# A two-layer graph network on one core: tables joined by pieces in the last stage, edge groups beside all second-layer tiles, 100 groups in the first pass

## Chip, cores and metric

The kernel runs on one core of one Trainium2 chip. The metric is the device time of one execution in microseconds; lower is better. Times below are from the profiled execution unless the three timed runs are named.

## What is computed

6250 nodes with 128 features, 206250 directed edges sorted by destination, each edge with a weight and 128 attributes.

```python
h = relu(layernorm(x))
# first layer: weighted sum over neighbours
deg = segment_sum(w, row); dinv = rsqrt(deg)
x = x + relu(segment_sum((dinv[row]*w*dinv[col])[:, None] * (h @ kernel)[col], row) + bias)
h = relu(layernorm(x))
# second layer: messages in both directions
fwd  = concat([h[src], edge_attr]) @ W_fwd  + b_fwd     # summed at dst
back = concat([h[dst], edge_attr]) @ W_back + b_back    # summed at src
agg = segment_sum(fwd, dst) + segment_sum(back, src);  agg = agg / (cnt + 1e-7)
y = leaky_relu(agg) + h
x = x + gamma * (y - mean(y)) * rsqrt(var(y) + 1e-5) + beta
```

The products with the weights are moved behind the sums, so the second layer needs, per node, the sum of `edge_attr` over its outgoing edges, the sum of `edge_attr` over its incoming edges, and the sums of `h` over its neighbours.

## The kernel before

**Edge groups.** The edges are cut into 202 groups of 1024 (`GE`, 8 steps of 128 edges). For each step VectorE (DVE) makes a 128x128 comparison of keys, TensorE (PE) multiplies it with the attributes, so that edges of the step with one source are summed, ScalarE (ACT) copies the result to SBUF, and GpSimd (POOL) issues one indirect DMA that adds 128 rows to a table in device memory. There are K = 4 tables (`d.tab_gcn`), used in turn, so a scatter waits for the one four before it. A row holds 256 words: 128 for the first layer's message sums, 128 for the attribute sums (`d.table(k)` is the second half).

**Two passes share the groups.** `first_layer` carries the first `G1` = 104 groups, and their scatters write both halves of a row (L879). It works in 26 half tiles of 64 node pairs: beside the 4 groups (`GPI`) of a half tile PE counts neighbours from one-hots (`pairs`, L1065), turns the counts of the half tile before (`turn`, L1043) and multiplies them with `g` (`product`, L1055), and DVE adds (L965). The order is written out: `slot` runs over 32 steps `c`, group work at each, turns at even ones, pairs at odd ones. Half tiles 0, 1 and 2 stand alone, then comes a loop over two at a time, then half tile 25 and a last slot without groups. `keep_sums` on ACT (L1102) may be two groups ahead of the scatters.

**The second pass.** `dense_sums` carries the other `NB` = 98 groups, whose scatters write the attribute half (L1742). It starts with `PG` = 6 groups beside the counting for tile 0 (32 batches of `pairs`) and the cutting of `h` into three bf16 parts (`cut_chunk`, five times, L1772). Then it runs over 25 tiles of 128 node pairs in 13 blocks: three products with the parts for each of 49 node tiles (L1934), the counting for the next tile (L1893), turns by DMA on ACT's queue (L1992), products back (L1956), adds on DVE (L1878), and beside them 4 groups (`GL`) per tile, 32 steps spread over the blocks. This is so for the first `BT` = 23 tiles; tiles 23 and 24 have no groups. `keep_sums` (L1971) fills a ring of four half groups. Each tile's row sums go out by ACT (L2033) and SP (L1707).

**Joining the tables.** When the last group is scattered, SP loads table 0 into `d.src_attr` (L1721 to L1724), and POOL adds tables 1, 2 and 3 to it by three DMAs that accumulate, each waiting for the one before (L1755 to L1760). `dense_sums` ends when they have landed.

**The last stage.** `last_nodes` works on 50 tiles of 128 nodes in five pieces of ten (`PT`). SP loads, per piece, `row_sums`, `h1` and `x1`, 640 KB each (L2192). PE turns a tile of `src_attr` (L2314) and makes five products into one bank (L2326 to L2335). DVE scales it (L2239), bends it (L2247), adds `h1` (L2256), and per piece takes the mean (L2261), variance (L2265), root and scale (L2270, L2271), and finishes (L2275, L2278). ACT squares and norms. POOL adds beta to `x1` (L2218), one instruction per piece. `load_sums` (L2119) belongs to a branch for other inputs that isn't taken.

## Time and profile before

| | us |
|---|---|
| three timed runs: median (lowest to highest) | 4065.53 (4058.59 to 4067.19) |
| profiled execution: its time | 4063.57 |
| profiled execution: its span | 4061.8 |
| first layer's scatters, first to last start | 443.3 to 2098.4 |
| second pass's scatters, first to last start | 2226.8 to 3824.6 |
| first work of the last stage on PE | 3936.4 |

A row of a timeline gives start, length, engine, line, operation, out<-in, count, and in brackets how long the engine had been idle and what released it. SPq and ACTq are DMA issues. `x832` is a count of instructions. POOL is busy in an indirect DMA while it writes its descriptors; the transfer itself lands later.

### The profile page before, as it was taken

What the parts mean: (1) busy time and instruction counts of PE and PEld (TensorE: products, weight loads), DVE (VectorE), ACT (ScalarE), POOL (GpSimd) and SP (SyncE); (2) the same over time, 40 slices, a digit from 0 to 9 for tenths busy, and PEclk for the clock granted to TensorE, in tenths of its full rate; (3) what the DMA queues carried; (4) which work ended last, traced back from release to release, by engine and by line L of the source; (5) the groups of instructions that cost most, each with busy time, mean ns of one, the idle gap of its engine ahead of it and who ended that gap; (6) DMA issues with size and microseconds to landing.
All of it is one profiled execution on the core that took longest, in us unless ns stands there. A gap on an engine that the chain in (4) does not pass through costs nothing. (4 is left out here: it accounts for less than half of the span.)

```text
span 4061.8 us, 95211 instructions
## 1 busy us (share of the span) xinstructions
PE 3260.1 (80%) x28078; PEld 2702.3 (67%) x28078; DVE 2860.3 (70%) x7842; ACT 1576.2 (39%) x4152; POOL 3035.7 (75%) x1814
## 2 busy tenths in 40 slices
PE   3455698888998889889964699888988889899836
PEld 2454587777777777777744577666766667667626
DVE  9899887777777778777846766666666666666515
ACT  1040455555555555555525233233332333333204
POOL 5778688888888888788850788888888888888610
PEclk9787899999999999999986599999999899999968
DMA  9980687877777778778779589888898989888992
GB/s 167 262 286 16 148 144 139 144 136 142 141 137 144 138 140 144 134 138 146 139 125 251 87 141 144 133 134 135 136 139 128 136 137 137 134 134 136 142 160 77
DMA packets 1032612, 582.11 MB, mean 143 GB/s; under 512 B 607653, under 2 KB 944074, under 8 KB 1032084
## 3 DMA queue, kind: packets, MB, share of 16 engines
q0 software_dynamic: 257584, 174.71, 38.0%
q1 hardware_dynamic: 450376, 320.42, 30.3%
q10 hardware_dynamic: 324124, 80.38, 13.1%
q8 instruction: 278, 4.55, 0.5%
q14 instruction: 250, 2.05, 0.2%
HBM read 282.86 MB, written 238.48 MB: 128 GB/s over the span
## 5 line engine op out<-in xcount | busy, mean ns | idle before, releaser
L1742 POOL DMA_INDIRECT gcn_sums<-shared x784 | 1344.8, 1715 | 381.5 <-issue 194.6
L879 POOL DMA_INDIRECT gcn_sums<-fl_sums,fl_to_i x832 | 1360.6, 1635 | 303.2 <-DMA gcn_sums<-fl_sums,fl_to_i 145.3
L1934 PE MATMUL bank<-ds_counts,ds_parts 128*128 128x256 bf16 x3675 | 620.3, 283 | 74.4 <-ACT ds_row_stage L2033 74.4
L1969 ACT CAST ds_counts<-bank 128x392 bf16<-128x392 f32 x800 | 387.6, 487 | 685.0 <-PE bank L1893 667.5
L1107 ACT COPY fl_sums<-bank 128x256 f32<-128x256 f32 x832 | 313.6, 377 | 603.8 <-PE bank L1034 376.9
L1934 PEld LDWEIGHTS bank<-ds_counts,ds_parts 128*128 128x128 bf16 x3675 | 362.4, 101 | 183.3 <-issue 84.8
L1956 PE MATMUL bank<-ds_turned,ds_now 128*128 128x512 bf16 (+1 forms) x1950 | 475.7, 382 | 7.9 <-DMA ds_turned<-ds_counts 7.4
L1913 PE MATMUL bank<-shared 128*128 128x128 f32 x1568 | 373.0, 322 | 25.2 <-DVE shared L1809 25.1
L917 DVE SCALAR_TENSOR_TENSOR fl_same<-fl_key_b,fl_pat,bank 128x128 f32<-128x128 bf16 x832 | 275.1, 343 | 155.1 <-PE bank L1034 138.6
L1033 PE MATMUL bank<-fl_pay,fl_same 128*128 128x128 f32 x1664 | 335.7, 284 | 50.5 <-issue 32.4
L1029 PEld LDWEIGHTS bank<-fl_sum_hot,fl_attrs 128*128 128x128 f32 x1664 | 253.0, 191 | 171.9 <-issue 108.7
L1911 PE MATMUL bank<-shared 128*128 128x64 f32 x1568 | 285.6, 287 | 95.1 <-DVE attr_sums L1796 93.9
L1878 DVE TENSOR_TENSOR src_sums<-src_sums,bank 128x512 f32<-128x512 f32 (+1 forms) x325 | 212.5, 654 | 209.1 <-PE bank L1956 204.6
L1029 PE MATMUL bank<-fl_sum_hot,fl_attrs 128*128 128x128 f32 x1664 | 311.9, 290 | 49.5 <-DVE attr_sums L902 49.4
L1055 PE MATMUL bank<-fl_turned,fl_g_tile 128*128 128x512 f32 (+1 forms) x676 | 336.9, 580 | 8.7 <-DVE gcn_t L965 7.7
L1065 PE MATMUL bank<-fl_hi_w,fl_lo_hot 128*128 128x98 bf16 x4992 | 287.7, 207 | 61.5 <-DVE fl_hi_w L956 59.3
L1034 PE MATMUL bank<-fl_attrs,fl_same 128*128 128x128 f32 x1664 | 326.8, 279 | 0.0
L956 DVE TENSOR_TENSOR fl_hi_w<-fl_hi_hot,fl_twos 128x784 bf16<-128x784 bf16 x624 | 316.6, 562 | 12.6 <-DVE fl_to_i L930 5.3
L1033 PEld LDWEIGHTS bank<-fl_pay,fl_same 128*128 128x128 f32 x1664 | 262.2, 194 | 91.5 <-issue 76.0
L965 DVE TENSOR_TENSOR gcn_t<-gcn_t,bank 128x512 f32<-128x512 f32 (+1 forms) x338 | 220.8, 653 | 132.8 <-PE bank L1055 129.6
L1893 PE MATMUL bank<-ds_hi_hot,ds_lo_hot 128*128 128x98 bf16 x3200 | 289.0, 214 | 30.2 <-issue 14.4
L1065 PEld LDWEIGHTS bank<-fl_hi_w,fl_lo_hot 128*128 128x128 bf16 x4992 | 256.5, 98 | 84.3 <-issue 69.4
(271 smaller groups left out, 6340.2 us busy)
## 6 DMA issues: line engine op xcount, KB each, us to landing
fl_attrs<-in_edge_attr SPq DMA_DIRECT2D x104, 512.0 KB, 4.7
shared<-in_edge_attr SPq DMA_DIRECT2D x194, 256.0 KB
fl_rel_b<-offset_rows SPq DMA_DIRECT2D x104, 256.0 KB
fl_key_b<-key_rows SPq DMA_DIRECT2D x104, 256.0 KB
gcn_sums<-zeros SPq DMA_DIRECT2D x40, 640.0 KB
shared<-key_rows SPq DMA_DIRECT2D x98, 256.0 KB
gcn_sums<-fl_sums,fl_to_i POOLq DMA_INDIRECT x832
near<-src_float SPq DMA_DIRECT2D x1, 12892.0 KB
```

The source lines that it names most:

```text
L879: nc.gpsimd.indirect_dma_start(out=d.tab_gcn[j % K], out_offset=bass.IndirectOffsetOnAxis(ap=to_i[:, (GPI * kk + gi) % 4, j:j + 1], axis=0 ...
L956: last = nc.vector.tensor_tensor(in_twos(hi_w[:, go % 2, m, :, :]), in_twos(hi_hot[:]), per_pair(hh, 2 + m, go, HH), ALU.mult)
L1029: nc.tensor.matmul(win_bank[:, 0:P], attrs[:, h, jj, :], sum_hot[:, jj, :], start=(jj == 0), stop=(jj == J - 1))
L1033: nc.tensor.matmul(sum_bank[j % 2][:, 0:F], same[:, j, :], pay[:, j // U, j % U, :], start=True, stop=True)
L1034: nc.tensor.matmul(sum_bank[j % 2][:, F:2 * F], same[:, j, :], attrs[:, h, j, :], start=True, stop=True).then_inc(summed, 1)
L1055: nc.tensor.matmul(prod_bank[:, 0:n], g_tile[:, old, :], turned[:, (old + b) % 2, 0:n], start=True, stop=True).then_inc(prod_ready, 1)
L1065: last = nc.tensor.matmul(pair_bank[:, c * HH:(c + 1) * HH], lo_hot[:, go % 2, q, :], hi_w[:, go % 2, m, q, :], start=(m == 0), stop=(m == 2))
L1742: nc.gpsimd.indirect_dma_start(out=d.tab_gcn[j % K].rearrange("n (two f) -> (n two) f", two=2), out_offset=bass.IndirectOffsetOnAxis(ap=to ...
L1913: nc.tensor.matmul(sum_bank[half][:, j % U * F:(j % U + 1) * F], same[:, j, :], attrs[:, half, j % U, :], start=True, stop=True).then_inc( ...
L1934: ins = nc.tensor.matmul(row_bank[:, 0:2 * P], parts[:, tile, s, :], counts[:, h, tile, :, :].rearrange("p b q -> p (b q)"), start=(tile = ...
L1956: ins = nc.tensor.matmul(back_bank[v][:, 0:n].rearrange("f (k p) -> f k p", p=P), now[:, h, half, s, :], by_half[:, half, :, :], start=(ha ...
L1969: nc.scalar.copy(to, pair_bank[batch % B][:, 0:PB * HH].rearrange("p (c k) -> p k c", c=PB)).then_inc(pair_copied, 1)
```

## The change

100 groups are in the first pass: half tiles 0, 1, 2 and 25 (`LIGHT`) have three groups, 24 steps, with the same turns, products and pairs spread over them. The second pass has 102 groups: 4 ahead of tile 0, 4 beside each of tiles 0 to 23, 2 beside tile 24. The join leaves `dense_sums`; POOL only waits there for its scatters. In `last_nodes` SP loads all four tables in pieces of 640 KB; DVE adds the first piece's three parts, POOL those of the other four pieces, each add waiting for the one before. `h1` and `x1` become rings of 3 and 4 pieces, so that there is room for six parts. PE waits for the adds at the first turn of each piece.

The groups' numbers:

```diff
-G1 = GPI * 2 * DS
+LIGHT = (0, 1, 2, 2 * DS - 1)
+G1 = GPI * 2 * DS - len(LIGHT)
 NB = NG - G1
 GL = 4
-PG = 6
-BT = (NB - PG) // GL
+PG = 4
+GL_LAST = NB - PG - GL * (SUPER - 1)
```

In `first_layer`:

```diff
+        def groups_in(i, kk):
+
+            if not isinstance(i, int):
+                return GPI
+            k = 2 * i + kk
+            return 0 if k == 2 * DS else GPI - 1 if k in LIGHT else GPI
...
+        def steps(i, kk):
+
+            return J * (groups_in(i, kk) or GPI)
+
+        def turn_at(i, kk, c):
+
+            return [b for b in range(BLOCKS + 1) if b * steps(i, kk) // BATCHES == c]
+
+        def pairs_at(i, kk, c):
+
+            return [n for n in range(BATCHES) if (2 * n + 1) * steps(i, kk) // (2 * BATCHES) == c]
...
-                for c in range(C):
+                for c in range(steps(i, kk)):
```

In `dense_sums`, the loop of every engine, SP and POOL:

```diff
-            with eng.Fori(1, BT // 2) as i:
...
-            pair_of_tiles(BT // 2, 0, True, False)
-            if between:
-                between()
-            pair_of_tiles(BT // 2, 1, False, False)
-            pair_of_tiles(SUPER // 2, 0, False, True)
+            tile(SUPER // 2 - 1, 0, False)
+            tile(SUPER // 2 - 1, 1, False)
+            tile(SUPER // 2, 0, True)
...
-            def load_table():
-                for k in range(K):
-                    sp.wait_ge(added[k], 16 * (J // K) * NB)
-                sp.dma_start(d.src_attr[:], d.table(0)).then_inc(first_in, 16)
...
-            pool.wait_ge(first_in, 16)
-            for k in range(1, K):
-                if k > 1:
-                    pool.wait_ge(merged, 16 * (k - 1))
-                nc.gpsimd.dma_start(d.src_attr[:], d.table(k), accum_op=ALU.add).then_inc(merged, 16)
-            pool.wait_ge(merged, 16 * (K - 1))
+            for gi in range(GL_LAST):
+                scatter_group(SUPER // 2, 0, gi)
+            for k in range(K):
+                pool.wait_ge(added[k], 16 * (J // K) * NB)
```

In `last_nodes`, in the order SP, POOL, DVE, PE:

```diff
+        ADDS = K - 1
+        PB = 2 * ADDS
...
+            def load_tables(r):
+                sp.dma_start(piece(d.src_attr, r), piece(d.table(0), r)).then_inc(acc_in[r], 16)
+                for k in range(1, K):
+                    n = r * ADDS + k - 1
+                    if n >= PB:
+                        before = n - PB + 1
+                        if before <= ADDS:
+                            sp.wait_ge(first_added, before)
+                        else:
+                            sp.wait_ge(later_added, before - ADDS)
+                    sp.dma_start(part[n % PB], piece(d.table(k), r)).then_inc(part_in[n % PB], 16)
...
+                at_least(sp, sum_ready, PT * (r - H1_RING + 1))
+                sp.dma_start(h1[:, r % H1_RING, :, :], piece(nodes(d.h1), r)).then_inc(h1_in[r], 16)
+                at_least(sp, out_ready, r - X1_RING + 1)
+                sp.dma_start(x1[:, r % X1_RING, :, :], piece(nodes(d.x1), r)).then_inc(x1_in[r], 16)
...
+            load_tables(0)
             for m, a in enumerate((d.w_back[F:2 * F, :], d.w_back[0:F, :], d.w_fwd[F:2 * F, :], d.w_fwd[0:F, :])):
                 sp.dma_start(w[:, m, :], a).then_inc(w_in, 16)
             load(0)
...
             for r in range(1, PIECES):
+                load_tables(r)
                 load(r)
...
+            def add_tables(r):
+                pool.wait_ge(acc_in[r], 16)
+                for n in range(r * ADDS, (r + 1) * ADDS):
+                    pool.wait_ge(part_in[n % PB], 16 * (n // PB + 1))
+                    nc.gpsimd.tensor_tensor(piece(d.src_attr, r), piece(d.src_attr, r), part[n % PB], ALU.add).then_inc(later_added, 1)
+                    pool.wait_ge(later_added, n - ADDS + 1)
+
             for r in range(PIECES):
+                if r + 1 < PIECES:
+                    add_tables(r + 1)
+                if r == 0:
+                    pool.wait_ge(bias_in, 32)
...
+            dve.wait_ge(acc_in[0], 16)
+            for n in range(ADDS):
+                dve.wait_ge(part_in[n], 16)
+                nc.vector.tensor_tensor(piece(d.src_attr, 0), piece(d.src_attr, 0), part[n], ALU.add).then_inc(first_added, 1)
+                dve.wait_ge(first_added, n + 1)
             dve.wait_ge(bias_in, 32)
...
+                if t == 0:
+                    pe.wait_ge(first_added, ADDS)
+                elif t % PT == 0:
+                    pe.wait_ge(later_added, ADDS * (t // PT))
```

The helpers `group`, `in_ring` and `loads` number the groups anew and keep the rings in step; every engine's loop uses them.

## Rows read from the trace of the kernel before

**Rows 1.** The page's first part: busy time of each engine over the span.
```profile
PE 3260.1 (80%) x28078; PEld 2702.3 (67%) x28078; DVE 2860.3 (70%) x7842; ACT 1576.2 (39%) x4152; POOL 3035.7 (75%) x1814
```

**Rows 2.** The view of line L879; min/median/max ns, first and last start; who waited.
```profile
L879 POOL DMA_INDIRECT gcn_sums<-fl_sums,fl_to_i x832: 1552/1567/2079, 443.3 to 2098.4; - x167
...
  ACT fl_sums L1107: 217.7, 158
```

**Rows 3.** Busy time by stretch, first layer: PE, PEld, DVE, ACT, POOL; granted clock, DMA.
```profile
1000.00:1300.00 300.00, 270.09 (x2467) 232.40 (x2466) 231.38 (x703) 161.78 (x439) 245.51 (x151) 0.98 0.78 137
```

**Rows 4.** The timeline of DVE where the first layer ends.
```profile
2101.56 0.29 DVE L965 TENSOR_TENSOR gcn_t<-gcn_t,bank 128x128 f32<-128x128 f32 x1 [0.64 <-PE bank L1055]
```

**Rows 5.** The view of line L1742, the second pass's scatters; who waited.
```profile
L1742 POOL DMA_INDIRECT gcn_sums<-shared x784: 1552/1567/2834, 2226.8 to 3824.6; - x196
...
  ACT shared L1981: 177.0, 93
```

**Rows 6.** The timeline of POOL: scatters 32 and 49 of the second pass.
```profile
2303.78 1.57 POOL L1742 DMA_INDIRECT gcn_sums<-shared  x1 [0.30 <-issue]
...
2337.97 1.55 POOL L1742 DMA_INDIRECT gcn_sums<-shared  x1 [0.30 <-issue]
```

**Rows 7.** The timeline of DVE: the fifth group is prepared while the fourth is summed.
```profile
2296.77 0.17 DVE L1813 SCALAR_TENSOR_TENSOR ds_to_f<-ds_later,ds_to_f 128x8 f32<-128x8 f32 x1
```

**Rows 8.** The view of line L1934: PE's products of tile 0 begin at 2312.9.
```profile
L1934 PE MATMUL bank<-ds_counts,ds_parts x3675: 269/273/421, 2312.9 to 3885.2; 128*128 128x256 bf16 x194
```

**Rows 9.** The timeline of ACT: first two half groups beside tile 0 copied out.
```profile
2325.76 0.59 ACT L1981 COPY shared<-bank 128x512 f32<-128x512 f32 x1
...
2333.59 0.59 ACT L1981 COPY shared<-bank 128x512 f32<-128x512 f32 x1
```

**Rows 10.** Busy time by stretch just before tile 0, columns as in group 3.
```profile
2280.00:2300.00 20.00, 11.54 (x63) 10.88 (x64) 14.28 (x39) 3.89 (x8) 16.33 (x9) 0.50 0.43 66
```

**Rows 11.** The timeline of ACT: ends of tiles 22, 23 and 24.
```profile
3797.25 0.37 ACT L2033 COPY ds_row_stage<-bank 128x256 f32<-128x256 f32 x1 [0.86 <-issue]
3840.41 0.37 ACT L2033 COPY ds_row_stage<-bank 128x256 f32<-128x256 f32 x1 [7.55 <-issue]
3885.53 0.37 ACT L2033 COPY ds_row_stage<-bank 128x256 f32<-128x256 f32 x1 [44.74 <-PE bank L1934]
```

**Rows 12.** The timeline of POOL: the last scatter and the last of three joins.
```profile
3824.61 1.57 POOL L1742 DMA_INDIRECT gcn_sums<-shared  x1 [0.30 <-issue]
...
3905.15 4.37 POOL L1759 DMA_DIRECT2D shared<-gcn_sums  x1 [22.55 <-DMA shared<-gcn_sums]
```

**Rows 13.** The timeline of SP and DVE: the last stage's first load and first scaling.
```profile
3936.81 2.18 SPq L2198 DMA_DIRECT2D n_w<-in_L_gnn_W_back  x2
...
3951.91 0.35 DVE L2239 TENSOR_SCALAR shared<-bank,n_per_count 128x128 f32<-128x128 f32 x1 [10.85 <-DMA n_per_feature<-in_L_gnn_beta]
```

**Rows 14.** The timeline of SP and DVE between the layers: same tables loaded in pieces.
```profile
2107.72 0.34 SPq L1417 DMA_DIRECT2D n_w<-in_L_gnn_kernel  x1
...
2118.14 1.49 DVE L1447 TENSOR_TENSOR n_acc<-n_acc,n_part 128x1280 f32<-128x1280 f32 x1 [9.66 <-DMA n_part<-gcn_sums]
...
2124.84 1.49 DVE L1447 TENSOR_TENSOR n_acc<-n_acc,n_part 128x1280 f32<-128x1280 f32 x1 [0.74 <-DMA n_part<-gcn_sums]
```

**Rows 15.** The view of line L2218, POOL's adds in the last stage.
```profile
L2218 POOL TENSOR_TENSOR n_x<-n_x,n_per_feature x5: 2887/2892/3059, 3951.9 to 3977.2; 128x1280 f32<-128x1280 f32 x5
```

**Rows 16.** The timeline of DVE, last stage: during and between POOL's adds.
```profile
3953.34 0.35 DVE L2239 TENSOR_SCALAR shared<-bank,n_per_count 128x128 f32<-128x128 f32 x1 [1.08 <-PE bank L2335]
3953.60 1.33 DVE L2247 SCALAR_TENSOR_TENSOR n_leaky<-shared 128x128 f32<-128x128 f32 x1
...
3962.22 0.27 DVE L2247 SCALAR_TENSOR_TENSOR n_leaky<-shared 128x128 f32<-128x128 f32 x1
...
3964.09 2.99 DVE L2256 SCALAR_TENSOR_TENSOR shared<-n_leaky,n_h 128x128 f32<-128x128 f32 x1
```

**Rows 17.** The view of line L2261, the mean of each piece.
```profile
L2261 DVE TENSOR_SCALAR n_stat<-n_stat x5: 172/173/173, 3968.5 to 4045.6; 128x10 f32<-128x10 f32 x5
```

More of the change, by code:

```diff
@@ L844, in slot @@
                 k = 2 * i + kk
-                for gi in range(0 if last else GPI):
-                    g, h = group(i, kk, gi), gi % 2
+                for gi in range(groups_in(i, kk)):
+                    g, h = group(i, kk, gi), in_ring(i, kk, gi) % 2
                     at_least(sp, to_ready, g - 1)
@@ L870, in slot @@
             def slot(i, kk, last):
-                for gi in range(0 if last else GPI):
-                    g, h = group(i, kk, gi), gi % 2
+                for gi in range(groups_in(i, kk)):
+                    g, h = group(i, kk, gi), in_ring(i, kk, gi) % 2
                     for j in range(J):
@@ L1072, in slot @@
                 first = isinstance(i, int) and i == 0
-                for c in range(C):
+                for c in range(steps(i, kk)):
                     gi, j = divmod(c, J)
@@ L1127, in slot @@
                 first = isinstance(i, int) and i == 0
-                for c in range(C):
+                for c in range(steps(i, kk)):
                     gi, j = divmod(c, J)
@@ L1573, in dense_sums @@
         U = 4
-        STEPS = GL * J
         RING = 4
@@ L1634, in dense_sums, with groups_in, steps_of @@
         wide = lambda b: min(HB, HI - b * HB)
-        def steps_of(b):
-            return range(STEPS * b // BLOCKS, STEPS * (b + 1) // BLOCKS)
+        def groups_in(i, h):
+            return GL_LAST if isinstance(i, int) and 2 * i + h == SUPER - 1 else GL
+        def steps_of(i, h, b):
+            n = J * groups_in(i, h)
+            return range(n * b // BLOCKS, n * (b + 1) // BLOCKS)
         def behind(i, h, gi):
@@ L1859, in _, with add @@
             dve.wait_ge(src_zeroed, CHUNKS)
-            def add(i, h, beside, last):
+            def add(i, h, last):
                 t = 2 * i + h
@@ L1918, in _, with products @@
                     pairs(0, 0, c, first=True)
-            def products(i, h, beside, last):
+            def products(i, h, last):
                 t = 2 * i + h
@@ L1925, in products @@
                     ahead = [] if last else list(range(3 * b, min(3 * b + 3, BATCHES)))
-                    steps = list(steps_of(b)) if beside else []
+                    steps = list(steps_of(i, h, b))
                     for k in range(wide(b)):
@@ L2005, in _, with copies @@
             keep_now(0, 0)
-            def copies(i, h, beside, last):
+            def copies(i, h, last):
                 t = 2 * i + h
@@ L2012, in copies @@
                     ahead = [] if last else list(range(3 * b, min(3 * b + 3, BATCHES)))
-                    steps = list(steps_of(b)) if beside else []
+                    steps = list(steps_of(i, h, b))
                     for n in range(max(len(ahead), len(steps))):
```

156 lines of the change are left out of this document (70 added, 86 removed).

## Prediction, made before the changed kernel ran

> **What bounds the kernel now.** The page's first part [rows 1] comes first: PE 80%, POOL 75%, DVE 70% of one span. Three engines so close say nothing yet, because the stages have different limits. So the views of the two scatter lines come next. In the first layer 832 scatters start from 443.3 to 2098.4 [rows 2]: 1655.1 / 831 = 1.992 us from one to the next, where the instruction alone has a median of 1.57. ACT, which may run two groups ahead, waited 217.7 us for scatters to land. PE is busy 270 of 300 us there [rows 3]: near its limit, but behind POOL. The second pass is alike: 784 scatters from 2226.8 to 3824.6, ACT waiting 177.0 us for them [rows 5]. POOL's queue of scatters sets both passes; a group of eight costs 8 x 1.992 = 15.9 us in the first.
>
> Behind the passes lies a stretch without scatters. The last ends at 3826.2 [rows 12], tile 22 had been finished by PE and ACT at 3797.3, tiles 23 and 24 follow at 3840.4 and 3885.5 [rows 11]. The joins go on: the last starts at 3905.15 [rows 12], and SP issues the last stage's first load at 3936.81 [rows 13]. From scatter to stage: 110.6 us, of which joins alone fill the last 51.
>
> **Part 1, four groups fewer in the first layer.** 4 x 15.9 = 63.7 us less if POOL stays the bound in the light half tiles. What they have besides groups (turns, products, pairs) is packed into 24 steps instead of 32. A half tile lasts 4 x 15.9 = 63.7 us and PE is busy in 0.90 of it, 57.4; the light one has 47.8 us of scatters. Half tile 0 has no turns or products, so PE can build its lead of two groups there, and that covers 1 and 2. After half tile 25 PE has a slot of turns and products without groups; DVE ended it at 2101.85 [rows 4], within 2 us of the last scatter's end at 2099.95, so what PE loses in this half tile shows. I take **-62**. Ends: -64 if PE never shows; if PE's 57.4 us did not shrink at all, each light half tile would save 6.3 and the four -25. ACT's and DVE's orders move with PE's and are bounded by the same two.
>
> **Part 2, the second pass.** Until its 32nd step the start is unchanged. The fourth group's last scatter ends at 2303.78 + 1.57 = 2305.35 [rows 6]. By 2296.8 DVE has prepared the fifth group [rows 7], which is now tile 0's first, so PE can begin tile 0 near 2297 and not at 2312.9 [rows 8]. The first half group of tile 0 was copied out at 2325.76 + 0.59, 13.4 us after tile 0's start, the next 7.8 us later [rows 8, 9]. So the fifth group's scatters begin near 2310.7, after 5.3 us of POOL with nothing; half groups every 7.8 us then feed a POOL that needs 8.1. The clock is granted at 0.50 before tile 0, that is 1.2 GHz, where PE had been busy 11.5 of 20 us [rows 10]; if tile 0's first blocks ran at half the pace, 13 us more would be lost.
>
> From scatter 49 at 2337.97 [rows 6] to 3826.2 are 92 groups: 16.18 us each. Now 98 groups start at 2310.7: 2310.7 + 98 x 16.18 = 3896.3. Tile 24 has two groups; alone it took 45.1 us [rows 11], and PE is 29 us ahead of the scatters at a tile's end (3826.2 - 3797.3), so its last half group is ready about when POOL has reached it. POOL's new wait at the end has nothing queued behind it but the stage's end. After the first layer's last scatter the next stage's first load came 7.8 us later (2107.72 - 2099.95) [rows 2, 14]; so here at 3904.1 instead of 3936.8: **-33**. SP loses one wait and one load. Ends: -38 with no idle POOL, -20 with the 13 us.
>
> **Part 3, the last stage.** Now SP issues four table loads ahead of everything. The same tables' other halves, in pieces of the same size, are joined between the layers: DVE's adds started at 2118.14 and, three later, at 2124.84 [rows 14], 2.23 us per piece. The first scaling on DVE came 15.1 us after the first load, waiting for gamma and beta at the end of the first loads [rows 13]; four pieces ahead make it 15.1 + 8.9 = 24.0. DVE's three adds of 1.49 (the fourth piece plus one add lands near 16) and PE's wait for them hide under that; all 50 tiles stand behind this wait, and they need gamma and beta anyway. So **+9**.
>
> Then POOL has 12 adds more. Its five adds of 2.89 us [rows 15] show what they cost DVE: an operation on two SBUF inputs that takes 0.27 took 1.33 and 2.99 while POOL was adding, ending as POOL did; scaling out of a bank went through in 0.35 beside it [rows 16]. The other three blocked operations lie between these, so 1.06 to 2.72 us lost per add.
>
> The Trainium skill (SBUF — State Buffer, the rules on engine contention) says that DVE with two SBUF inputs and a GpSimd instruction that reads SBUF share a port pair by an exclusive lock, held for the whole instruction of whichever comes first. By that rule every new add could block DVE for all its length, 12 x 2.89 = 34.7 us, an estimate from the rule and the row; this speaks against moving the adds to POOL.
>
> The rows have DVE free part of the time. A piece of the stage is seven loads, 7 x 2.23 = 15.6 us; POOL works 4 x 2.89 = 11.6 of them, from about +28 to +88 after the first load. In each add one tile gets through DVE (one bend, one sum between two adds); in the 4 free us about three: 7 tiles per 15.6 us, and with the five operations per piece besides, near 27 us a piece. Now a piece takes (4045.6 - 3968.5) / 4 = 19.3 [rows 17]. In 60 us: 2.2 pieces instead of 3.1, so 0.9 x 19.3 = **+17**. Ends: 0, if the idle time of DVE in the 19.3 swallowed it all, and 12 x 3.06 = +37. SP's waits for part buffers are for adds a piece earlier, and the h1 and x1 rings wait for pieces three and four earlier; behind them are only loads of pieces that DVE reaches later. Loads at 15.6 a piece stay ahead of DVE.
>
> **Sum.** -62 - 33 + 26 = -69 us on the profiled execution's 4063.6: 3994.6. Its span is 4061.8, 1.8 less; the three runs' median is 4065.5, 1.9 more. Against the median: **3996.5**. Some 8 us (0.2%) is what a measurement of this kernel can tell from no change.
>
> **Rivals.**
> - *Light half tiles give less.* PE, busy in 0.90 of the time [rows 3], becomes their bound. For it: 57.4 of 63.7 us. Against: only a quarter of the groups leaves, and the lead covers three of four. At half the gain, -31: 4027. Chance 0.13.
> - *The lock costs all it can.* +9 + 37 instead of +26: 4016. For it: the 2.99 row; against: the 1.33 row. Chance 0.17. This is the outcome under the skill's rule above.
> - *DVE's idle time swallows the adds.* +9 alone: 3979. For it: POOL finished its adds at 3980 and the stage went on to 4062 at an unchanged 19 us per piece. Chance 0.14.
> - *Slower: the adds stretch.* Place: POOL in the last stage, the last-stage pieces waiting on the adds. POOL's add now has two full pieces as inputs, where one was a broadcast row, and each adds' successor waits for it. Parts 1 and 2 gain 95 and the start costs 9, so it decides at 86 / 12 = 7.2 us per add on the path; at 10 us, +120, the time is 4065.5 - 95 + 9 + 120 = 4100. Against: 2887 to 3059 ns in all five [rows 15]. Chance 0.03.
> - *The groups are moved and nothing else.* A group costs 15.9 in one pass and 16.2 in the other, and if the freed half tiles gave nothing (part 1 at -10) the rest is -33 + 26: 4049. Chance 0.03.
>
> **Numbers.** The forecast has 0.50. Ends: part 1 -64 to -25, part 2 -38 to -20, part 3 +9 to +46; all at once 3972.5 and 4066.5. The range 3972 to 4032 holds the forecast, the lock, the swallowed adds and half-gained half tiles, leaving out the corner where several ends meet. Faster by over 0.2%: 0.93; within: 0.03; slower: 0.04.
>
> **What will show it.** Right: L879's scatters at 1.99 us apart and ending some 62 us earlier; a POOL gap of about 5 us before scatter 33 of the second pass; the last stage's first load about 8 us after the last scatter; first scaling near +24; long L2247 and L2256 operations wherever POOL adds, and early pieces near 27 us apart, late ones near 19. Wrong: gaps on L879 that end with ACT in half tiles 0 to 2 or 25; a longer gap at tile 0; PE waiting for a load or for an add at a piece's first turn; POOL adds longer than 3.1 us.

## The result and the profile after

The changed kernel takes 4034.3 us (median of six runs, 4022.1 to 4044.3), the kernel before 4059.7 in the same runs: ratio 0.9934, 95% interval 0.9917 to 0.9951. It is faster, but by 0.7% and not by the 1.7% forecast; 4034.3 lies just above the range. The profiled execution took 4032.6 us with a span of 4030.6, 31.2 less than before; the forecast for that difference was 69. Times of the experiments below are medians of four executions, with the lowest and the highest, unless one execution is named; one of e13's four took 9519.5 us and is left out of its figures.

The first part of the page has the same three busy engines [rows 1]:

```profile
PE 3246.0 (81%) x27950; PEld 2693.9 (67%) x27950; DVE 2890.0 (72%) x7841; ACT 1576.3 (39%) x4096; POOL 3030.5 (75%) x1823
```

The first layer's scatters are now line L904. Its view in the changed kernel (instruction, then what its idle time ended with, then who waited for it):

```profile
L904 POOL DMA_INDIRECT gcn_sums<-fl_sums,fl_to_i x800: 1552/1553/2077, 445.8 to 2055.2; - x160
...
  issue: 161.4, 473
  ACT fl_sums L1135: 98.2, 130
...
  ACT fl_sums L1135: 50.1, 78
```

Against [rows 2]: ACT's waiting for scatters has fallen from 217.7 to 50.1 us, and POOL sits 98.2 us idle until ACT has copied a sum. The queue of scatters has stopped being the bound; the chain through PE is. The layer's last add, by the timeline of DVE:

```profile
2078.42 0.29 DVE L990 TENSOR_TENSOR gcn_t<-gcn_t,bank 128x128 f32<-128x128 f32 x1 [0.64 <-PE bank L1082]
```

Against 2101.56 [rows 4] that is 23.1 us earlier, where the last scatter came 43.2 earlier: before, DVE's last add stood within 2 us of the last scatter's end, now 22 us behind it. The timeline of POOL, from the first layer's last scatter to the last stage:

```profile
2055.16 1.55 POOL L904 DMA_INDIRECT gcn_sums<-fl_sums,fl_to_i  x1 [0.30 <-issue]
...
2198.80 1.55 POOL L1765 DMA_INDIRECT gcn_sums<-shared  x1 [142.08 <-ACT shared L1999]
...
2282.11 1.55 POOL L1765 DMA_INDIRECT gcn_sums<-shared  x1 [4.23 <-ACT shared L1999]
...
3860.91 1.55 POOL L1765 DMA_INDIRECT gcn_sums<-shared  x1 [0.30 <-issue]
...
3898.59 3.04 POOL L2242 TENSOR_TENSOR shared<-shared,n_part 128x1280 f32<-128x1280 f32 x1 [24.36 <-DMA n_part<-gcn_sums]
...
3913.69 8.94 POOL L2242 TENSOR_TENSOR shared<-shared,n_part 128x1280 f32<-128x1280 f32 x3 [2.91 <-DMA n_part<-gcn_sums]
...
3945.45 11.23 POOL L2242 TENSOR_TENSOR shared<-shared,n_part 128x1280 f32<-128x1280 f32 x3 [4.01 <-DMA n_part<-gcn_sums]
3956.75 5.91 POOL L2251 TENSOR_TENSOR n_x<-n_x,n_per_feature 128x1280 f32<-128x1280 f32 x2
```

So the second pass begins at 2198.8 and not 2226.85: 28.1 us are what is left of part 1 there. Its scatters end at 3862.5; the last stage's first load comes 8.7 us later, by SP's timeline:

```profile
3871.19 0.41 SPq L2200 DMA_DIRECT2D shared<-gcn_sums  x1
```

From the first scatter of the pass to that load are 1672.4 us, where 1710.0 lay before (3936.81 - 2226.85): 37.6 less. From there to the end of the span: 159.4, before 125.0: 34.4 more. Sum: -28.1 - 37.6 + 34.4 = -31.3. The last stage by the timeline of DVE: first scaling (after the wait for gamma and beta), two tiles beside POOL's adds, the mean of each piece (L2294), and a scale (L2304) and a finish (L2311) beside adds:

```profile
3894.03 0.61 DVE L2272 TENSOR_SCALAR shared<-bank,n_per_count 128x128 f32<-128x128 f32 x2 [7.10 <-DMA n_per_feature<-in_L_gnn_beta]
...
3898.78 2.99 DVE L2289 SCALAR_TENSOR_TENSOR shared<-n_leaky,n_h 128x128 f32<-128x128 f32 x1
...
3901.70 0.34 DVE L2272 TENSOR_SCALAR shared<-bank,n_per_count 128x128 f32<-128x128 f32 x1
3901.97 2.76 DVE L2280 SCALAR_TENSOR_TENSOR n_leaky<-shared 128x128 f32<-128x128 f32 x1
...
3916.97 2.72 DVE L2294 TENSOR_SCALAR n_stat<-n_stat 128x10 f32<-128x10 f32 x1
...
3932.92 2.59 DVE L2304 TENSOR_TENSOR n_stat<-n_stat 128x10 f32<-128x10 f32 x1
...
3945.70 2.73 DVE L2294 TENSOR_SCALAR n_stat<-n_stat 128x10 f32<-128x10 f32 x1
...
3949.86 4.08 DVE L2311 TENSOR_TENSOR shared<-shared,n_x 128x1280 f32<-128x1280 f32 x1
...
3977.42 0.17 DVE L2294 TENSOR_SCALAR n_stat<-n_stat 128x10 f32<-128x10 f32 x1
...
3997.20 0.17 DVE L2294 TENSOR_SCALAR n_stat<-n_stat 128x10 f32<-128x10 f32 x1
...
4014.37 0.17 DVE L2294 TENSOR_SCALAR n_stat<-n_stat 128x10 f32<-128x10 f32 x1
```

The first scaling comes 22.8 us after the first load (15.1 before); the pieces then stand 28.7, 31.7, 19.8 and 17.2 us apart, 19.3 on average before [rows 17].

### The profile page after: what moved, and what is told of

Same layout as the page of the kernel before. It is cut to its first block and busy times, and to the rows that moved or that the text cites. A ratio compares the mean times of both kernels' runs of the same rounds, so it can differ in the third digit from the quotient of the medians.

```text
span 4030.6 us, 94845 instructions
## 1 busy us (share of the span) xinstructions
PE 3246.0 (81%) x27950; PEld 2693.9 (67%) x27950; DVE 2890.0 (72%) x7841; ACT 1576.3 (39%) x4096; POOL 3030.5 (75%) x1823
## 5 line engine op out<-in xcount | busy, mean ns | idle before, releaser
L1765 POOL DMA_INDIRECT gcn_sums<-shared x816 | 1392.1, 1706 | 413.7 <-issue 200.0
L904 POOL DMA_INDIRECT gcn_sums<-fl_sums,fl_to_i x800 | 1282.9, 1604 | 335.3 <-issue 161.4
L1135 ACT COPY fl_sums<-bank 128x256 f32<-128x256 f32 x800 | 300.5, 376 | 498.8 <-PE bank L1061 438.9
L1931 PE MATMUL bank<-shared 128*128 128x128 f32 x1632 | 381.3, 317 | 23.0 <-DVE shared L1827 20.9
L942 DVE SCALAR_TENSOR_TENSOR fl_same<-fl_key_b,fl_pat,bank 128x128 f32<-128x128 bf16 x800 | 264.9, 342 | 165.6 <-PE bank L1061 149.5
L1929 PE MATMUL bank<-shared 128*128 128x64 f32 x1632 | 295.2, 285 | 91.1 <-DVE attr_sums L1814 89.9
L1060 PE MATMUL bank<-fl_pay,fl_same 128*128 128x128 f32 x1600 | 322.5, 284 | 38.8 <-issue 38.3
L1061 PE MATMUL bank<-fl_attrs,fl_same 128*128 128x128 f32 x1600 | 315.5, 280 | 0.0
L1929 PEld LDWEIGHTS bank<-shared 128*128 128x128 f32 x1632 | 243.4, 201 | 103.3 <-DVE attr_sums L1814 100.4
L990 DVE TENSOR_TENSOR gcn_t<-gcn_t,bank 128x512 f32<-128x512 f32 (+1 forms) x338 | 220.7, 653 | 126.1 <-PE bank L1082 125.0
L647 PE MATMUL bank<-col_w,row_hot 128*128 128x200 bf16 x1616 | 188.4, 288 | 152.2 <-DVE col_w L560 152.2
```

What stands on the lines that cost most here:

```text
L904: nc.gpsimd.indirect_dma_start(out=d.tab_gcn[j % K], out_offset=bass.IndirectOffsetOnAxis(ap=to_i[:, in_ring(i, kk, gi), j:j + 1], axis=0) ...
L1060: nc.tensor.matmul(sum_bank[j % 2][:, 0:F], same[:, j, :], pay[:, j // U, j % U, :], start=True, stop=True)
L1765: nc.gpsimd.indirect_dma_start(out=d.tab_gcn[j % K].rearrange("n (two f) -> (n two) f", two=2), out_offset=bass.IndirectOffsetOnAxis(ap=to ...
L1929: nc.tensor.matmul(win_bank[:, 0:W], attrs[:, jj // U, jj % U, :], sum_hot[:, jj, :], start=(jj == 0), stop=(jj == J - 1))
L1931: nc.tensor.matmul(sum_bank[half][:, j % U * F:(j % U + 1) * F], same[:, j, :], attrs[:, half, j % U, :], start=True, stop=True).then_inc( ...
```

## The experiments

Half tiles are measured on POOL, from the first scatter of one to the first of the next (us), the last of them to the end of its last scatter. "Even" and "odd" are the means over the full half tiles 6, 8, ... 24 and 5, 7, ... 23; the loop over two half tiles turns ahead of every odd one. "Layer" runs from the first scatter to DVE's last add. Second stop: does PE stand still twice at a turn of the loop (below)?

| kernel (light half tiles) | 0 | 1 | 2 | even | odd | 25 | layer | second stop |
|---|---|---|---|---|---|---|---|---|
| before (none) | 66.8 | 65.4 | 62.6 | 64.2 | 63.3 | 60.3 | 1658.5 | no |
| before, again: r1 | 65.4 | 62.9 | 63.6 | 63.6 | 63.7 | 60.6 | 1653.0 | no |
| changed (0, 1, 2, 25) | 52.4 | 50.8 | 53.2 | 62.4 | 65.7 | 49.8 | 1632.9 | yes |
| e1 (1, 2, 25) | 65.5 | 46.4 | 47.6 | 63.2 | 62.4 | 45.7 | 1601.6 | no |
| e2 (none) | 65.4 | 62.0 | 61.9 | 63.1 | 62.2 | 60.3 | 1633.0 | no |
| e8 (2, 25) | 65.2 | 63.0 | 46.3 | 63.0 | 65.4 | 47.8 | 1654.2 | yes |
| e5, one-hots earlier | 48.8 | 46.9 | 48.6 | 63.2 | 64.7 | 45.9 | 1611.3 | yes |
| e10, 32 transposes | 52.9 | 50.3 | 53.3 | 63.3 | 63.0 | 45.6 | 1606.9 | no |
| e15, 64 transposes | 48.5 | 51.2 | 53.3 | 63.0 | 63.4 | 45.0 | 1602.7 | no |
| e16, 16 transposes | 50.1 | 50.7 | 53.3 | 62.9 | 66.7 | 49.1 | 1646.4 | yes |
| e13, as e5 and e10 together | 50.9 | 46.4 | 47.5 | 62.5 | 63.1 | 45.7 | 1591.1 | no |
| e18, e6 and 72 transposes | 62.8 | 47.0 | 47.1 | 63.3 | 66.8 | 46.5 | 1654.8 | yes |
| e19, 128 transposes | 47.7 | 51.2 | 53.3 | 62.8 | 66.0 | 49.1 | 1635.0 | yes |

**Which half tiles are light (e1, e2, e8).** The theory at that point: without a full half tile 0, PE has no lead over the scatters. The edit, with the counts that hang on it (the 3 in `group`, `in_ring` and `loads` becomes the number of light half tiles ahead of the loop; tiles 23 and 24 of the second pass share what is left):

```diff
-LIGHT = (0, 1, 2, 2 * DS - 1)
+LIGHT = (1, 2, 2 * DS - 1)      # e1; () in e2, (2, 2 * DS - 1) in e8
```

> Half tile 0 of the first layer gets its fourth group back (light half tiles 1, 2 and 25; 101 groups in the first layer, 101 in the second pass, one of them beside the last tile). My theory: in the changed kernel PE and DVE, not the scatters, set the pace of half tile 0 (three groups in 53.1 us there, four in 53.8 us in the kernel before), so the fourth group costs the first layer about 1 us and takes 16 us out of the second pass: about 15 us less than the changed kernel, 4017 against its profiled 4032, with the first layer's last DVE add within 2 us of 2078.7. Rival, the scatters bind it as forecast: the group costs 15.9 us there and saves 16.2 us here: 4032, the first layer ending near 2094.

e1 took 3995.4 us (3991.4 to 3998.7; ratio to before 0.9858, 0.9832 to 0.9884): one group more in the first layer, and the layer is 31 us shorter. Its light half tiles last 46.4, 47.6 and 45.7 us: the 47.8 that the forecast gave for one. So the price of a light half tile was right, as long as a full one stands ahead of it. But the gain (39 us) is more than twice the 15 that my theory expected, so something else went with it.

> Part 1 undone: no light half tiles, 104 groups in the first layer as before; 98 in the second pass, with four ahead, four in each of tiles 0 to 22, two in tile 23 and none in tile 24. My theory: the first layer ends some 23 to 28 us later than in the changed kernel, near 2102 to 2106, as in the kernel before; the second pass's scatters end some 65 - 25 = 40 us earlier, but tiles 23 and 24 then stand alone on PE (45 us each in the trace of before), so the last stage begins within 5 us of where it begins now: 4032 +- 8. Rival, each group was worth 15.9 us in the first layer: it ends near 2078.7 + 62 = 2141 and the whole takes some 35 us longer, 4067.

e2 took 4009.1 us (3991.8 to 4011.6; 0.9892, 0.9866 to 0.9917): 25 us less than the changed kernel with part 1 undone, outside both expectations. So in this kernel the four groups were better left in the first layer. Two steps of mine failed. Tile 24 without groups took PE 32 us and not 45. And the first layer took 1633.0 us with instructions that are the same on every engine as in the kernel before; the repeat, r1, says that the kernel before has 1653 to 1658 in two profiles.

> The kernel before once more, unchanged, for one more profile: the run without light half tiles has the same instructions in its first layer, yet took 1633.0 us from the first scatter to the last DVE add where the profile of before shows 1658.5. If executions differ in the pace of the scatters, this one lies anywhere from 1630 to 1665, its full half tiles near 62.6 to 63.7 us; if something in the changed kernel's placement makes it faster, it is 1655 to 1662 again.

r1: 4059.2 us (one execution), layer 1653.0, within its broad expectation. Executions differ (e2's profiled one was 16 to 20 us faster than its other three), but there is more to it. Between 660 and 2000 us the scatters stand 1.99 us apart in both profiles of the kernel before and 1.96 in e2; in the kernels below with light half tiles it is 1.96 to 1.97 where the loop has one stop at a turn, and 1.98 and 1.99 with four half tiles to a turn (e3, e9). So a full half tile differs by up to 1 us from kernel to kernel without a light half tile in it, the layer by some 20 us. Why the same instructions ran quicker in e2 was not settled.

> Half tiles 2 and 25 alone are light: one group is taken out ahead of the loop (an odd number, as the three of the changed kernel), and half tile 0 is full; 102 groups in the first layer, 100 in the second pass, none of them beside tile 24. Theory, it is the light half tile 0 that costs PE's lead: the full half tiles last 62 to 64 us without alternating, the first layer ends 14 to 16 us after that of the kernel with 1, 2 and 25 light (2043.9), near 2059; the second pass is up to 16 us shorter, less what tile 24 shows alone: 3993 to 4006. Rival, the odd number makes the half tiles alternate: 62 and 67, the first layer ending near 2085, the whole above 4015.

e8 took 4025.8 us (4017.4 to 4029.7; 0.9924, 0.9907 to 0.9940), the rival's outcome. Half tile 0 is full, and yet from half tile 13 on the odd ones last 66 to 69 us. So a lead is built, and then something uses it up. What that is stands in PE's waits between 660 and 2000 us (total, times, longest), here in the changed kernel:

```profile
PE bank L1060 <- issue: 38.3, 10, 5.0
...
PE bank L1092 <- issue: 16.7, 10, 2.6
```

in the kernel before

```profile
PE bank L1033 <- issue: 32.4, 10, 3.6
```

and in e8

```profile
PE bank L1063 <- issue: 43.7, 10, 5.0
...
PE bank L1046 <- issue: 21.9, 10, 3.1
```

Ten turns of the loop, ten stops in which PE waits for nothing that the profile shows. The kernel before has one of 3.2 us at each turn; the changed kernel and e8 have a second one a few us behind it. In PE's timeline of the changed kernel:

```profile
976.40 0.48 PE L1060 MATMUL bank<-fl_pay,fl_same 128*128 128x128 f32 x2 [3.37 <-issue]
976.72 0.39 PE L1061 MATMUL bank<-fl_attrs,fl_same 128*128 128x128 f32 x2
976.94 0.78 PE L1070 MATMUL bank<-ident,fl_mat 128*128 128x128 f32 x4
977.51 0.64 PE L1060 MATMUL bank<-fl_pay,fl_same 128*128 128x128 f32 x2
977.94 0.63 PE L1061 MATMUL bank<-fl_attrs,fl_same 128*128 128x128 f32 x2
978.37 1.91 PE L1043 MATMUL bank<-fl_window,fl_spread_hot 128*128 128x128 f32 x8
980.08 0.62 PE L1092 MATMUL bank<-fl_hi_w,fl_lo_hot 128*128 128x98 bf16 x5
983.29 0.48 PE L1092 MATMUL bank<-fl_hi_w,fl_lo_hot 128*128 128x98 bf16 x7 [2.60 <-issue]
```

2 + 2 + 4 + 2 + 2 + 8 + 5 = 25 matmuls after the turn PE stops again, within a run of twelve that wait for nothing. Two theories: the odd number of groups taken out (three, one) shifts the pairs of groups against the half tiles; or PE's code stands in another place.

**The loop's turns (e3, e10, e11, e14 to e19).**

```diff
-            with eng.Fori(2, DS) as i:
-                slot(i, -1, False)
-                slot(i, 0, False)
+            slot(2, -1, False)
+            slot(2, 0, False)
+            with eng.Fori(0, (DS - 3) // 2) as two:
+                for i in (2 * two + 3, 2 * two + 4):
+                    slot(i, -1, False)
+                    slot(i, 0, False)
```

> The changed kernel with four half tiles to a turn of the first layer's loop, not two, so that the loop turns 5 times and not 11. Theory: with half tile 0 light, PE and DVE have no lead over the scatters, and the 3 to 5 us that PE stands still at each turn of the loop show; six turns fewer take 15 to 30 us off the first layer (DVE's last add near 2050 to 2064, not 2078.7), the whole 4004 to 4019. Rival, the full half tiles alternate between 62 and 67 us because an odd number of groups was taken out ahead of the loop, so that pairs of groups straddle half tiles: the alternation stays, the first layer ends within 5 us of 2078.7.

e3 took 3982.9 us (3976.3 to 3991.3; 0.9820, 0.9797 to 0.9842), the layer 1598.7: more than expected, because the four stops that are left between 660 and 2000 us are single, and the alternation is gone with an odd number still taken out. That speaks against the odd number. The next edit changes nothing but the place of PE's code; its result is not used:

```diff
+            for _ in range(32):     # 64, 16, 128 in e15, e16, e19; 72, 16 in e18, e17
+                nc.tensor.transpose(turn_bank[:, 0:P], d.ident[:], d.ident[:])
             spread(0, 0, 0, 0)
```

> The changed kernel with 32 transposes more on PE ahead of the first layer, whose result is not used, in time in which PE waits. They move the code of PE's loop by as many instructions as one group has: its turn then stands where it stands in the kernel with half tiles 1, 2 and 25 light. Theory, the place of the loop's code decides whether PE stands still once (3.3 us) or twice (4 + 2.5 us) at each turn: full half tiles last 62 to 64 us without alternating, the first layer gets 20 to 30 us shorter (1603 to 1613, not 1632.9), the whole 4003 to 4014. Rival, the odd number of groups taken out makes them alternate, whatever the place: 4030 +- 8 and the alternation as before.

e10 took 4013.8 us (4008.0 to 4020.0; 0.9899, 0.9878 to 0.9921): 20 us less than the changed kernel, for 32 useless transposes. The layer is 26.0 us shorter, the odd half tiles last 63.0. Its waits have one stop per turn (no second row for matmuls that wait for "issue"):

```profile
PE bank L1060 <- issue: 38.9, 10, 4.6
```

> The kernel with half tiles 1, 2 and 25 light and the adds on DVE, with the same 32 transposes ahead of the first layer, which put PE's loop where it stands in the kernel with 2 and 25 light. Theory, place of the code: PE stands still twice at each turn, the lead over the scatters shrinks until the half tiles alternate between 63 and 67 us, the first layer takes 1615 to 1632 us, not 1604.8, the whole 3986 to 4004, not 3976. Rival, odd number of groups: two were taken out, so nothing changes: 3976 +- 5.

e11 took 3977.3 us (3973.5 to 3988.6) beside 3976.4 without the transposes: no change, the rival's outcome. So place alone, as I had counted it (by groups of 32 matmuls), was wrong; four more shifts tell what the place means.

> The kernel with half tiles 2 and 25 light (one group taken out ahead of the loop; PE stood still twice at each turn, 65.2 us in all stops of 1.6 us or more) with the 32 transposes ahead. If the place of PE's loop decides in every kernel that takes an odd number out, as it did in the changed kernel: one stop per turn, some 40 us in all, no alternation, the first layer 1620 to 1632 us, not 1654.2. If the changed kernel was an exception: two stops, 1650 again.

> The changed kernel with 64 transposes ahead, not 32. If what counts is the place of the loop in blocks of 64 PE instructions, this is where the changed kernel stood: two stops a turn, the alternation, the first layer 1625 to 1640 us. If any shift away from the changed kernel's place helps (or the 7 us of PE work ahead does): one stop, 1600 to 1613.

> The changed kernel with 16 transposes ahead. Half way between the two places: if the second stop appears gradually with the place, stops of some 45 us in all and a first layer of 1610 to 1625 us; if it is there or not, either 1600 to 1613 or 1625 to 1640.

> The kernel with half tiles 1, 2 and 25 light and the adds on DVE, with 16 transposes ahead. Where an even number of groups is taken out, a shift by 32 had changed nothing. If no place matters there: one stop per turn of 2.7 to 3.9 us, first layer 1600 to 1610. If it was only that place: a second stop, first layer 1615 to 1630.

One execution each. e14: 3994.2 us, one stop, layer 1619.8. e15: 4016.3, one stop, layer 1602.7. e16: 4056.2, two stops, the second one 11 matmuls behind the turn and not 25, layer 1646.4, 6 us above its range. e17: 3981.4, one stop, layer 1607.2. PE's timeline of e16 behind a turn:

```profile
720.32 0.79 PE L1060 MATMUL bank<-fl_pay,fl_same 128*128 128x128 f32 x2 [4.06 <-issue]
720.90 0.63 PE L1061 MATMUL bank<-fl_attrs,fl_same 128*128 128x128 f32 x2
721.33 1.06 PE L1070 MATMUL bank<-ident,fl_mat 128*128 128x128 f32 x4
722.18 0.63 PE L1060 MATMUL bank<-fl_pay,fl_same 128*128 128x128 f32 x2
722.61 0.42 PE L1061 MATMUL bank<-fl_attrs,fl_same 128*128 128x128 f32 x1
726.97 0.58 PE L1061 MATMUL bank<-fl_attrs,fl_same 128*128 128x128 f32 x1 [3.93 <-issue]
```

That ruled out blocks of 64 PE instructions, and gave a scale: 16 transposes move the second stop 14 matmuls closer to the turn; with 32 and 64 it is gone. In the traces a transpose is two instructions, a weight load and a matmul. In e8 the second stop stands 14 matmuls behind the turn. From this the last two runs were foretold:

> The kernel with half tiles 1, 2 and 25 light and the adds on DVE, with 72 transposes ahead. Theory: PE's code comes in blocks of 256 instructions (a transpose is two, a load of weights and a matmul), and a block that ends within the first 30 matmuls of the loop costs a second stop at each turn. In the changed kernel the second stop lies 25 matmuls behind the turn, with 16 transposes ahead 11, with 2 and 25 light (two groups more) 14: so a group is some 139 instructions, here the end lies 83 matmuls behind the turn, and 72 transposes bring it to about 11 (5 to 17). Two stops per turn, over 55 us in all, half tiles alternating between 63 and 67, the first layer 1615 to 1635 us and a start up to 8 us later. Rival, an even number taken out never shows it: one stop, 1600 to 1610.

> The changed kernel with 128 transposes ahead, that is 256 instructions. Theory: the same place in a block as without them: two stops per turn, the second 25 matmuls behind the turn (21 to 29), the alternation, some 1625 to 1640 us from the first scatter to the end of the first layer, its start up to 20 us later. Rival, any shift of more than 16 removes it: one stop, 1600 to 1613.

In both the second stop came, close to the place foretold; e18's layer did not stay in its range. e18, an even number taken out, PE's timeline behind a turn:

```profile
1112.61 0.79 PE L1063 MATMUL bank<-fl_pay,fl_same 128*128 128x128 f32 x2 [4.64 <-issue]
1113.19 0.63 PE L1064 MATMUL bank<-fl_attrs,fl_same 128*128 128x128 f32 x2
1113.62 1.06 PE L1073 MATMUL bank<-ident,fl_mat 128*128 128x128 f32 x4
1114.47 0.63 PE L1063 MATMUL bank<-fl_pay,fl_same 128*128 128x128 f32 x2
1114.89 0.63 PE L1064 MATMUL bank<-fl_attrs,fl_same 128*128 128x128 f32 x2
1118.55 1.86 PE L1046 MATMUL bank<-fl_window,fl_spread_hot 128*128 128x128 f32 x7 [3.02 <-issue]
```

The second stop stands 12 or 13 matmuls behind the turn (the stretch shows seven of eight matmuls of L1046), 11 foretold; the odd half tiles last 66.8, the layer 1654.8, 50 us more than without the transposes (20 more than I had allowed), the kernel 4026.6. e19, with 256 instructions ahead, is back at the changed kernel's place; its timeline:

```profile
1241.82 0.38 PE L1092 MATMUL bank<-fl_hi_w,fl_lo_hot 128*128 128x98 bf16 x5
1244.97 0.76 PE L1092 MATMUL bank<-fl_hi_w,fl_lo_hot 128*128 128x98 bf16 x7 [2.77 <-issue]
```

again after five of the twelve, 25 matmuls behind the turn; layer 1635.0, kernel 4047.2. So the place of PE's loop counts, with a period of 256 instructions: a shift by 256 brings the second stop back to its matmul, shifts by 64 and 128 (e10, e15) do not. That PE's code comes in pieces of 256, and that each turn costs a second stop where a piece ends shortly behind the start of the loop, is the reading that foretold both runs; no trace shows the pieces themselves. An odd or even number has no part in it, nor has the work of the transposes: e19 has the most of it and gains nothing.

**One step of slack in the light half tiles (e5).** With three groups, DVE's weighing stands one step ahead of the pairs on PE that use it, with four, two. In half tile 0 of the changed kernel (450 to 496 us) PE's waits say:

```profile
PE bank L1092 <- DVE fl_hi_w L981: 8.9, 7, 3.1
```

```diff
-                        if not last and c == full * (go - 1) + full - 2:
+                        if not last and c == full * (go - 1) + full - (2 if full == GPI else 3):
                             one_hots(k, hh, go)
-                        if not last and c == full * (go - 1) + full - 1:
+                        if not last and c == full * (go - 1) + full - (1 if full == GPI else 2):
```

> In the four light half tiles alone DVE builds each set of one-hots one step earlier, so that between the weighing and the pairs on PE that use it lie two steps, as in a full half tile, and not one. Theory, PE and DVE wait for each other in turn in the light half tiles (PE waited 8.9 us for the weighing in half tile 0): each light half tile gets 3 to 8 us shorter, half tile 0 going from 52.4 to about 46; the first layer ends 10 to 25 us earlier, the whole is 10 to 25 us less, 4008 to 4022. Rival, PE's own work (47 us busy in a light half tile) and the loop behind it set the end: less than 4 us.

e5 took 4009.8 us (4007.6 to 4010.3; 0.9890, 0.9864 to 0.9915): 24.5 less than the changed kernel, as the theory had it, and the same row in that stretch:

```profile
PE bank L1092 <- DVE fl_hi_w L981: 2.5, 3, 1.1
```

In half tiles 1 and 2 PE's wait for the weighing goes from 4.6 and 4.7 us to nothing, and they last 46.9 and 48.6 us, not 50.8 and 53.2. In half tile 0 the clock comes in as well. From 466 to 472 us the changed kernel's PE has the granted clock 0.50, the lower of its two levels (1.2 GHz), after 6 us in which it was busy for 2.9; e5 has 1.00 (columns as in [rows 3], the changed kernel first):

```profile
466.00:472.00 6.00, 6.00 (x43) 5.94 (x44) 2.74 (x10) 1.55 (x4) 3.33 (x3) 0.50 0.87 215
466.00:472.00 6.00, 5.60 (x66) 5.09 (x63) 5.04 (x18) 4.22 (x14) 5.03 (x3) 1.00 0.79 128
```

Over the whole of half tile 0 the mean clock is 0.88 in the changed kernel (52.4 us) and 0.96 in e15 and e19, which wait as long for the weighing (10.3 to 10.8 us in each of the three) and need 48.5 and 47.7. So the weighing explains half tiles 1 and 2, but not half tile 0's 52.4.

**The last stage (e4, e6).** e4 leaves the twelve adds out; e6, on top of e1, gives them to DVE:

```diff
-                    nc.gpsimd.tensor_tensor(piece(d.src_attr, r), ..., ALU.add).then_inc(later_added, 1)
+                    pool.sem_inc(later_added, 1)                                   # e4
...
+                if at in (6, 7) and r + 1 < PIECES:                                # e6
+                    for k in ((0,) if at == 6 else (1, 2)):
+                        add_table((r + 1) * ADDS + k)
```

> The twelve adds of POOL in the last stage are left out (the loads stay; tables 1 to 3 of pieces 1 to 4 are not added). Theory, the adds hold DVE: from the first scaling to the end goes from 136.6 us back to about 112 (109.9 before the change), the whole 25 us less than the changed kernel: 4007. Rival, the twelve pieces more to be loaded set the pace (15.6 us a piece) or PE's wait for a piece: from the first scaling to the end stays above 125, the whole above 4020.

e4 took 4001.6 us (3999.8 to 4012.2; 0.9879, 0.9850 to 0.9908). From first scaling (3889.9) to the end of the span (3998.8): 108.9, the changed kernel 136.6. All of the growth there is the adds, 27.7 / 12 = 2.3 us each; the twelve pieces more that are still loaded cost nothing behind the first scaling. That the adds cost their time by holding DVE shows in its timeline: added up over the stage, DVE's operations that run beside an instruction of POOL last 38.4 us longer than the same ones alone, before the change 9.4.

> On top of the kernel with half tile 0 full (light: 1, 2, 25): DVE makes the twelve adds of the last stage, one after tile 6 and two after tile 7 of the piece before, where it waited 1.4 and 3.6 us for PE; POOL keeps the five adds of beta. Theory, POOL's adds hold DVE by a lock and DVE's waits can take in most of 12 x 1.49 us: from the first scaling to the end 112 to 118 us, not 136.3; the whole 3971 to 3977. Rival, DVE's own 18 us show in full: 126 to 130, the whole 3985 to 3990.

e6 took 3976.4 us (3974.9 to 3979.8; 0.9801, 0.9784 to 0.9817), 19 less than e1; from first scaling to the end 114.0. Twelve adds of 1.49 us cost 5 us more than no adds (e4), put where DVE waits for PE anyway.

**Versions that beat both (e9, e13).** e9 is e6 with e3's loop; e13 is the changed kernel with e5's, e10's and e6's edits.

> The kernel with half tiles 1, 2 and 25 light and the adds on DVE, with four half tiles to a turn of the first layer's loop. Theory, PE's lead at the end of the first layer covers the slot of turns and products behind the last group (27 us from the last copied sum to the last add): with six turns fewer the lead grows from 11 to some 18 us, the first layer takes 1592 to 1600 us, not 1604.8, the whole 3963 to 3972. Rival, the scatters hold PE back anyway: 3976 +- 4.

> The changed kernel's four light half tiles with DVE's one-hots a step earlier in these, the 32 transposes ahead of the first layer, and the last stage's adds on DVE. Theory, the three gains add up: first layer 1580 to 1592 us, last stage from its first scaling to the end near 116, the whole 3962 to 3976. Rival, without the lead of a full half tile 0 PE still sets the end: first layer above 1600, the whole above 3980.

e9 took 3969.5 us (3962.4 to 3974.0), ratio 0.9786 (0.9762 to 0.9810): 2.1% below the kernel before. Its layer took 1608.4, not shorter than e6's 1604.8, so the gain is not where I expected it; over e6 the difference (7 us) is within the spread of e9's own executions (12 us). e13 took 3965.6 to 3982.7 us; its ratio is 0.9778 (0.9753 to 0.9803), the same within the intervals; its layer of 1591.1, within its expectation, is the shortest.

## Why the prediction was wrong

The miss is 69 - 31 = 38 us on the profiled execution: 34 in part 1, 8 in part 3, and 5 the other way in part 2 (each rounded).

**Part 1, -62: wrong; -28 at the second pass's first scatter.** The scatters' price held: where the scatters bind, a light half tile takes 46 to 48 us (e1, e13). The step that failed is "Half tile 0 has no turns or products, so PE can build its lead of two groups there, and that covers 1 and 2". Half tile 0 is one of those made light, and ended with no lead: in half tiles 1 and 2 POOL stood idle for 14.1 us until ACT had copied a sum, 0.9 before the change, and they took 50.8 and 53.2 us. The four light half tiles together gave 49 us, not 64. A second term had 2 us in the forecast (64 - 62) and measured 20: PE's lead also pays for the stops at the loop's turns, and for the slot of turns and products at the layer's end. I had read PE as "busy 270 of 300" [rows 3] and not looked at what its idle time was; ten stops of 3.2 us are in it. The change shortened the code ahead of the loop, a second stop came to each turn, and between 660 and 2000 us POOL waited 64.1 us for copied sums, where it had waited 36.0 (25.1 in e10). PE reached the last slot without a lead: DVE's last add stands 22.0 us behind the end of the last scatter, before 1.9; the full half tiles took 3 us more.

Without the second stop the layer takes 1602.7 to 1606.9 us (e15, e10), 26 to 30 less than the changed kernel; with the one-hots a step earlier as well, 1591.1 (e13). That is 62 to 67 less than the two profiles of the kernel before, but only 42 less than e2, which has all 104 groups in its first layer: so how much of it the light half tiles gave is known to some 20 us only. Against e2 the scatters of e13 take 55 us less, near the forecast, and 13 of these are lost again at the end, where the last slot shows for 18.4 us and not 5.2. Against the same e2 the changed kernel's light half tiles gave its first layer nothing (1632.9 and 1633.0; e2's profile is of its fastest execution).

**Part 2, -33: right, -37.6.** The gap ahead of scatter 33 of the pass is 4.23 us (5.3 forecast), the first load 8.7 us behind the last scatter's end (7.8). I had taken the 8.1 us per half group of before; the pass ran at about that.

**Part 3, +26: the mechanism was right, the size not; +34.4.** The start is +7.7 (forecast +9). The lock is +26.7, where the forecast had +17 and, as its upper end, 37. Each add cost 2.3 us, within the 1.06 to 2.72 of the rows. The mis-sized term is the pace of 27 us a piece while POOL adds. From first scaling to the end of the last add beside it are 68.6 us (3894.0 to 3962.7; I gave it 60), in which 42 us of the stage got done (68.6 - 26.7): 31.5 us for what takes 19.3 without the adds. That these are the forecast's 2.2 pieces is chance; the longer stretch alone, at 27 us a piece, would have made +20. The forecast let a tile pass with every add and counted the five operations per piece at their own length. In the timeline four of the twelve adds held such an operation instead: two means (2.72 and 2.73 for 0.17), a scale (2.59 for 0.17) and a finish (4.08 for 1.49), 10 us together. The lock works in both directions: three adds of POOL's took 11.23 where three others took 8.94, beside DVE's 4.08 for the finish, an add of 1.49. The Trainium skill (SBUF — State Buffer, on engine contention) says that whichever starts first holds the ports for its whole instruction and the other waits; the rows agree, also in that scaling out of a bank took its 0.34 beside an add. Its rule, all adds blocking for their length, gave 34.7; the measured 27.7 is nearer to that than to my 17.

**The rivals.** "Light half tiles give less" came nearest, 4027, and PE was their bound, as it says. But 49 of the 64 us came in the light half tiles themselves, and the 20 us at the layer's end are not in it. The lock at its worst (4016) bears on 8 of the 38 us, the swallowed adds are out by e4, and POOL's adds did not stretch to 7.2 us (4.10 at most, from 2.88). That the groups are moved and nothing else is nearer to the truth than its chance of 0.03: against the kernel before, four of them gave 28 us, 7 each, and against e2 nothing. With the obstacles gone a light half tile is worth some 16 us where it stands (46 to 48 us beside 62 to 63), and in the layer's end 10 for each group, measured against e2.

## What to carry to other kernels

Work taken out of the first unit of a pipeline is also taken out of the time in which the engine behind builds its lead; look at what that lead pays for (a loop's turn, the slot at the end) before counting on it. When the code ahead of a loop changes length, look at the stops right behind the loop's turn in the engine's timeline: a second one may have appeared, and instructions ahead of the loop, in time in which the engine waits, can move it away; how many has to be tried (here 32 and 64 transposes did it, 16 and 128 did not). Before a gain is put down to a change, measure it against a kernel that has everything but this change (here e2), not against the old one alone. An add that has to be made somewhere is cheapest in the gaps of the engine that would otherwise be blocked by it.

## What was not expected of the hardware

That 32 matmuls whose result nobody reads make a kernel 20 us faster (e10), and 72 make another one 50 us slower (e18). PE stands still for 3.2 to 4.5 us on average at each turn of the first layer's loop, and in the kernels with a second stop for 1.5 to 2.6 us more, 11 to 25 matmuls behind the turn. In e11, where by the count in e18's expectation a piece of 256 instructions ends some 50 matmuls behind the turn (an estimate), no second stop shows. The Trainium skill (Advanced Engine Details and Errata, section ISA Cache) says that code is cached in lines of 256 instructions; the shift by 128 transposes, after which the stop was back 25 matmuls behind the turn, agrees with the 256. What stays open is why the first layer of e2 took 20 to 25 us less than in two profiles of the kernel before with the same instructions.
